# Attention and mixture-of-experts kernel: times-v matmuls of each pair in two blocks of two chunks, output and v projections one place later

## What is computed

```python
q, k, v = (einsum('bsd,hdk->bhsk', x, w) for w in (w_q, w_k, w_v))      # 16 heads of 64
weights = softmax(einsum('bhqk,bhmk->bhqm', q, k) / 8, axis=-1)         # 512 x 512 for each head
z = einsum('bhqm,bhmk->bhqk', weights, v)
x = layernorm(x + x + concat_heads(z) @ w_o)
# then 8 experts 128 -> 256 -> 128 with silu, the two best of each token, weighted
x = layernorm(x + x + experts(x))
```

## Time and profile before

| | |
|---|---|
| median of 3 runs | 1280.31 us (1279.3 to 1281.87) |
| profiled execution, span | 1280.0 us |
| PE (matmul) busy | 1196.7 us, 93% |
| DVE busy | 987.7 us, 77% |
| POOL busy | 679.6 us, 53% |
| ACT (ScalarE) busy | 602.0 us, 47% |
| pair 32 starts its scores at | 602.44 us |
| pair 33 | 617.67 us |
| pair 34 | 631.92 us |

### The profile page before, as it was taken

One profiled execution on the slowest core, in us unless ns is written; L12 is line 12 of the kernel. 1 busy time (PEld: TensorE's weight loads), 2 busy tenths in 40 slices (PEclk: granted clock), 3 DMA queues, 4 the chain that ended last, 5 costly groups with the idle time before them and its releaser, 6 DMA issues. The chain is left out here.

```text
span 1280.0 us, 20247 instructions
## 1 busy us (share of the span) xinstructions
PE 1196.7 (93%) x4952; PEld 693.9 (54%) x4952; DVE 987.7 (77%) x1618; ACT 602.0 (47%) x744; POOL 679.6 (53%) x502
## 2 busy tenths in 40 slices
PE   5799999999999999999999999999998788888886
PEld 3454555555555555555555555555553566666664
DVE  4586888788888788888788888788887667777764
ACT  4444444444444444444444444444443555556553
POOL 0464644455544455544555544555546366666665
PEclk9898999999999999999999999999999889999999
DMA  9666666566665565665666665656660000000000
GB/s 213 162 161 153 157 155 157 144 156 147 157 156 140 144 155 146 158 159 153 150 150 153 159 148 140 150 149 152 160 161 21 21 9 17 17 17 16 8 9 17
DMA packets 91643, 153.47 MB, mean 120 GB/s; under 512 B 18016, under 2 KB 36960, under 8 KB 91616
## 3 DMA queue, kind: packets, MB, share of 16 engines
q1 hardware_dynamic: 91616, 153.14, 48.1%
HBM read 6.30 MB, written 2.10 MB: 7 GB/s over the span
## 5 line engine op out<-in xcount | busy, mean ns | idle before, releaser
L1025 DVE TENSOR_REDUCE neg_max<-psum 128x1 fp32r<-128x512 f32 x512 | 345.1, 680 | 114.1 <-PE psum L530 112.1
L1040 DVE RECIPROCAL zT<-zT 128x128 f32<-128x128 f32 x256 | 241.4, 944 | 4.2 <-ACT zT L865 2.2
L530 PE MATMUL psum<-k_stack,q_stack 128*128 128x512 f32 x512 | 224.6, 451 | 6.8 <-DVE neg_max L1025 1.4
L555 PE MATMUL psum<-q_stack,k_stack 128*128 128x512 f32 x512 | 210.5, 411 | 9.9 <-DMA q_stack<-q_stack 7.4
L858 ACT ACTIVATE probs_even<-psum 128x1024 f32<-128x1024 f32 x128 | 131.0, 1023 | 179.1 <-PE psum L556 179.1
L556 PE MATMUL psum<-q_stack,k_stack 65*128 65x512 f32 x512 | 205.2, 401 | 0.0
L396 POOL TENSOR_TENSOR probs_sum<-probs_even 128x512 f32<-128x512 f32 x64 | 82.5, 1289 | 227.4 <-PE psum L581 187.2
L396 POOL TENSOR_TENSOR probs_sum<-x_tok 128x512 f32<-128x512 f32 x64 | 82.2, 1284 | 226.9 <-PE psum L581 226.9
L530 PEld LDWEIGHTS psum<-k_stack,q_stack 128*128 128x128 f32 x512 | 97.1, 190 | 185.0 <-DVE neg_max L1025 87.9
L396 POOL TENSOR_TENSOR probs_sum<-probs_sum,probs_even 128x512 f32<-128x512 f32 x128 | 164.1, 1282 | 14.5 <-ACT probs_even L858 3.3
L396 POOL TENSOR_TENSOR probs_sum<-probs_sum,x_tok 128x512 f32<-128x512 f32 x128 | 164.3, 1283 | 11.3
(11 more groups left out here) (119 smaller groups left out, 1927.1 us busy)
## 6 DMA issues: line engine op xcount, KB each, us to landing
q_stack<-q_pair SPq DMA_DIRECT2D x128, 256.0 KB, 3.0
k_stack<-k_pair SPq DMA_DIRECT2D x128, 256.0 KB, 3.6
q_stack<-q_pair SPq DMA_DIRECT2D x128, 128.0 KB, 3.5
k_stack<-k_pair SPq DMA_DIRECT2D x128, 128.0 KB, 3.4
xT_cur<-xT SPq DMA_DIRECT2D x32, 512.0 KB, 3.0
wqk_cur<-w_tab SPq DMA_DIRECT2D x63, 256.0 KB, 3.3
wo_cur<-w_tab SPq DMA_DIRECT2D x64, 128.0 KB, 3.0
x_tok<-L_attn_x_dram SPq DMA_DIRECT2D x8, 256.0 KB, 5.4
```

The source lines that it names most:

```text
L530: nc.tensor.matmul(psum[:, COARSE + t % 2, :], q_stack[j][:, h, 0, t * P:(t + 1) * P], k_stack[j][:, h, 0, :], start=True, stop=True).then ...
L555: nc.tensor.matmul(psum[:, t, :], k_stack[j][:, h, 0, keys], q_stack[j][:, h, 0, :], start=True, stop=False)
L1025: nc.vector.tensor_reduce(neg_max[h][:, t:t + 1], psum[:, COARSE + t % 2, :], AX.X, ALU.max, negate=True).then_inc(s["max_done"], 1)
L1040: nc.vector.reciprocal(zT[:, cols], zT[:, cols]).then_inc(s["r_done"], 1)
```

## The change

Only PE's list is changed. In each body the four chunks of `times_v` stood at four places with a coarse matmul between them; they now stand at two places, chunks 0 and 1 with `sum_probs` behind them, and chunks 2 and 3. Coarse (0,2) comes after the first block. In the second half `project_out` and `project_v` move one place later: `project_out` stands after coarse (1,1) and `project_v` after coarse (1,2).

```diff
                 next_coarse(0, 1)
                 if former:
                     times_v(n - 1, 1 - j, 0)
-                next_coarse(0, 2)
-                if former:
                     times_v(n - 1, 1 - j, 1)
                     sum_probs(n - 1, 1 - j)
+                next_coarse(0, 2)
                 next_coarse(0, 3)
...
                 next_coarse(1, 0)
                 if former:
                     times_v(n - 1, 1 - j, 2)
+                    times_v(n - 1, 1 - j, 3)
+                next_coarse(1, 1)
                 if before_former:
                     project_out(n - 2)
-                next_coarse(1, 1)
+                next_coarse(1, 2)
                 if j == 0:
                     project_v(n)
-                next_coarse(1, 2)
-                if former:
-                    times_v(n - 1, 1 - j, 3)
                 next_coarse(1, 3)
```

## The result

| | before | changed |
|---|---|---|
| median | 1281.09 us (1279.3 to 1283.95, 4 runs) | 1327.05 us (1326.35 to 1327.77, 4 runs) |
| profiled span | 1280.0 us | 1325.7 us |

The ratio is 1.0354, with a 95% interval of 1.0338 to 1.0371. The change costs 46 us; I had said 33, with 1325 as the upper end of the range. The direction and the place were right, and the size was too small by 13 us.

The account below looks back on a forecast made before the run. PE was taken as the bound by a small margin, with DVE late at certain points. Thirty times +1.10 us gave +33.0, less 0.6 for pairs 1 and 63: 1312.4, stated as 1313 us, eight in ten 1300 to 1325.

Parts of the forecast that it names:

- The passages: PE's switches between plain fp32 and fp32r matmuls: 0.30 us per block, 0.60 us a pair saved if nothing waits.
- The first half, +0.16 us a pair: Late coarse (0,2) delays maxima (0,2) and (0,3), so the transpose waits: +0.16 us a pair, bounds -0.21 to +0.3.
- The even second half, -0.24 us: Even pairs: project_v fills most of coarse (1,3)'s wait, leaving 0.06 us; the next pair starts 0.24 us sooner.
- The odd second half, +0.92 us: Odd pairs, without project_v: PE waits 1.48 us before coarse (1,3); +0.79 to +1.05 us, middle +0.92.
- The chain of 1.94 us: From project_out's last matmul through DVE's addition and maximum (1,1) to coarse (1,3): 1.94 us, which cannot shrink.
- The copy of v, +0.10 us: ScalarE's copy of v, now after the later project_v, delays the second scores: +0.1 us per odd pair, 0 to 0.3.
- SP and POOL, nothing: SP's weight reload waits 1.16 us longer but its k stacks are needed later; POOL gets sums earlier: no cost.
- The clock, a rival with a chance of 0.05 and 102 us: The odd pair's wait drops the granted clock, 3.4 us lost thirty times: 1415 us; chance 0.05.
- pair 1, which I had gaining 0.3: Pair 1 has no project_out and gains some 0.3 us from fewer blocks.
- three twos: A two is an even and an odd pair, put at +1.10 us; pairs 2 to 61 make thirty, +33.0 us.
- The passages count and the waits do not: Rival: fewer fp32/fp32r switches save time and the odd pair has no wait; 1243 us, chance 0.04.
- the gain and the waits cancel: Rival: all bounds at their good end, +0.13 us for two pairs, 1284 us, no change; chance 0.02.

Follow-up runs that it names:

- The experiment with the first half alone: Kernel before with only chunks 0 and 1 and the sums in one block, coarse (0,2) behind them; 1296.64 us, ratio 1.0128.
- second half alone: Kernel before with only chunks 2 and 3 in one block, project_out and project_v one place later; 1316.23 us, ratio 1.0267.
- the last experiment: PE's list of the fastest kernel, with DVE's addition L1061 back ahead of maximum (1,1) as in the kernel before; 1375.67 us, ratio 1.0717.
- the one with the addition later: Changed kernel with maximum (1,1) moved ahead of the addition in DVE's list, PE's list untouched; 1299.98 us, ratio 1.0144.
- the fastest: Against before: two-chunk blocks, coarse (0,2) and (1,1) ahead of them, project_out after project_v, DVE's addition just ahead of maximum (1,3); 1249.66 us, ratio 0.9747.
- its second half alone: Kernel before with coarse (1,1) early, chunks 2 and 3 in one block, project_out last, DVE's addition later; first half unchanged; 1262.71 us, ratio 0.9845.
- the sums last: The fastest kernel's second half; first half chunks 0 and 1, coarse (0,2), coarse (0,3), then sum_probs; 1257.26 us, ratio 0.9807 against before.

## Why the prediction was right in kind and wrong in size

Step by step, with two pairs in the middle of the loop as the measure (forecast 1.10 us more, measured 1.44 at full clock):

- **The passages.** A chunk followed by more fp32 steps at 0.91 us and one block less saves 0.30 us of PE's time: right. Chunks 2 and 3 with their ways in and out took 625.90 - 623.70 = 2.20 us, and I had 2.25.
- **The first half, +0.16 us a pair.** The mechanism was right, the size was not. From coarse (0,1) to the transpose it is 637.47 - 632.26 = 5.21 us against 4.93 in the earlier trace rows, +0.28. I had let the sums start 0.07 behind the end of q's low part; they start 634.58 - (633.75 + 0.68) = 0.15 behind it, and the step out of them is 635.59 - 634.58 = 1.01 in place of the 0.96 that I took from a block that had not waited. The odd pair, read by its whole first half, is 0.24 longer. Measured for the two: 0.51, not 0.32. The experiment with the first half alone has 0.47.
- **The even second half, -0.24 us.** 644.56 - 639.27 = 5.29 against 5.47: -0.18. Coarse (1,3) steps at 0.34, not 0.23.
- **The odd second half, +0.92 us.** The chain of 1.94 us and the wait of coarse (1,3) were right to some hundredths (1.31 us idle in the record; 1.71 from one coarse matmul to the next, which is 1.48 over a step of 0.23, as forecast). What was off was the step from coarse (1,3) to the next pair. I had it at 0.36: 0.23 for the matmul and 0.13, half of the turn of the loop, on the thought that PE's sequencer might get the turn done in the wait. It is 629.24 - 628.64 = 0.60, that is 0.34 for a matmul that has waited, as in the even half, and the whole turn of 0.26. Measured +1.10. I had read the Trainium skill ("Perfetto Trace Analysis", Sequencer Loop) as putting the turn inside the wait; the trace shows the contrary: the turn's branch on PE comes behind the wait (last section).
- **The copy of v, +0.10 us.** Nothing of it is seen: ahead of its place the odd pair does not wait longer than before.
- **SP and POOL, nothing.** No wait of PE on the stacks of k appeared in the loop.
- **The clock, a rival with a chance of 0.05 and 102 us.** Neither right nor wrong as I had put it: a wait of 1.3 us does drop the clock, but in 2 of some thirty rounds, at 1.25 us each. The sum had nothing for it, and it cost 2.5 us. I should have added it to the sum with a small weight in place of treating it as all or nothing.

Together: 0.34 us more in two pairs makes 9.2 us over the 27 rounds of the loop, the clock 2.5, and pair 1, which I had gaining 0.3, loses 0.4 (14.10 us against 13.68). The rest, 0.9, lies in pair 0, for which I had nothing (13.76 us against 13.44), and behind pair 61. That is the missing 13 us. The pairs 2 to 7 of the straight code, where there is no turn and the wait is 1.15 us, cost 3.3 us, as much as I had put for three twos. The step that failed is the sum's sizing of two terms: the first half, put at 2 x 0.16 and measured 0.51, and the odd second half, put at +0.92 and measured +1.10, for the step across the turn. In both I took the kinder value where the rows left it open; the unkind one, 0.10 for the copy of v, went the other way and took some of the error back. "The passages count and the waits do not" and "the gain and the waits cancel" are out: the waits of L530 and L537 are in the trace, and moving the addition takes the first of them away without a change to PE's list.

## What to carry to other kernels

When two engines run hand-written lists in order, a move on one list has to be checked against the other's order: look for the first instruction over there that waits for what you move, and for what you yourself need from behind it. Here regrouping PE's work costs 3.5% or gains 2.5% with the same blocks, depending on one addition's place in DVE's list, on which coarse matmuls go ahead of the blocks and on how late `project_out` comes. Where an engine is 93% busy, the other engine's idle share says nothing about the slack at a given point. A wait just ahead of the turn of a loop costs more than its own length, since here the turn is hidden only where PE has not waited.

## What was unexpected of the hardware

- The granted clock fell behind waits shorter than the 2.45 us of the earlier trace rows, and not each time. With an odd pair's wait of 1.3 us, 2 of some thirty even pairs behind it were slow (changed kernel) and 6 (second half alone), with 1.1 us one, with 1.55 us 14 of 26. Kernels without the wait had none in the middle of the loop. In the last experiment the even pairs end with the same 1.55 us wait, and the odd pairs behind it are never slow (15.30 to 15.32 us). What differs in the trace is that the turn of the loop follows the odd pair's wait (a step of 621.22 - 620.62 = 0.60) and not the even pair's (637.83 - 637.49 = 0.34); whether that is the reason is not shown.
- The turn of the loop costs PE 0.26 us only if PE has waited just ahead of it. In eight of the eleven kernels, before and changed among them, coarse (1,3) of the odd pair waits for DVE (in the one with the addition later by a few hundredths alone), and the step from it to the next pair is 0.59 to 0.65 us across the turn, against 0.34 in the straight code, here in the changed kernel:

```profile
131.65 0.50 PE L530 MATMUL psum<-k_stack,q_stack 128*128 128x512 f32 x1 [1.15 <-DVE neg_max L1023]
131.98 0.40 PE L555 MATMUL psum<-q_stack,k_stack 128*128 128x512 f32 x1
```

  In the three kernels whose second half does not wait (the fastest, its second half alone, the sums last) that step is 0.23 to 0.24 in the loop, with the turn and without. The branch shows why: L186 on PE's sequencer, which the profile calls PEldq. It takes 215 ns in both kinds (minimum, median and maximum, then the first and the last start), first in the changed kernel and then in the fastest:

```profile
L186 PEldq COMPARE_BRANCH  x1: 215/215/215, 628.7 to 628.7; - x1
...
L186 PEldq COMPARE_BRANCH  x1: 215/215/215, 610.5 to 610.5; - x1
```

  In the changed kernel it comes behind coarse (1,3) at 628.64, and PE has nothing to do until it and the register instructions behind it are through: the sequencer did not go on while that matmul waited. In the fastest kernel it comes half a microsecond ahead of coarse (1,3) at 610.99, while PE still works on `project_out`.
- Plain fp32 and fp32r matmuls cost some 0.10 us at the way in, at the last fp32 chunk and at the first fp32r matmul behind it. Of this, what falls between two chunks is gone where fp32 follows fp32: two chunks in one block step at 1.87 us (609.96 - 608.09 in the fastest kernel) where two separate ones take 2 x 1.01. The 0.10 behind a block is not peculiar to fp32: an fp32r matmul that has waited for DVE steps at the same 0.34 us (644.56 - 644.22 in the changed kernel).
